# Transformer layer in 32 steps: a value half and a second-FFN piece trade places on TensorE, two low halves of squares move one slot later on VectorE

## The chip, the cores and the metric

The program runs on one core of one Trainium2 chip. The metric is the device time of one execution in microseconds (us), the median of several runs. The engines are named as in the profile: PE is TensorE's matrix multiply, PEld its load of the stationary operand, DVE is VectorE, ACT is ScalarE, POOL is GpSimd and SP the queue that issues transfers.

## What is computed

One transformer layer on 8 sequences of 1024 rows of width 512, with a sliding window of 256 keys, 16 heads of 32, and a feed-forward network (FFN) of 2048 hidden units whose weights are ternary and have a low-rank addition:

```python
x = L0_attn_x
x = x + _layernorm(_L0_attn_ref(_layernorm(x, axis=-1), Wq, bq, Wk, bk, Wv, bv, Wo, bo), axis=-1)
x = x + _layernorm(_L0_ffn_ref(_layernorm(x, axis=-1), fast_b, w_fc, w_proj, u, v, gate), axis=-1)
# _L0_ffn_ref:
h = _bitlinear(x, w_fc) + gate * (x @ v.T @ fast_b.T @ u.T)
r = jnp.maximum(h, 0.0)
return _bitlinear(r * r, w_proj)
```

## The kernel before

The 8192 rows are cut into 32 steps of 256 rows, four steps to a sequence; step t is the (t % 4)-th of its sequence, and the first of each sequence has no earlier keys. Every engine runs the same loop, `run_iterations`: iterations -2 to 34, each of 32 slots. A slot is the unit of order: in each slot every engine issues what the tables name for it, in the order in which its `body` is written, and the engines meet only through semaphores. The tables map a slot number of 0 to 95 to a piece of work; the number modulo 32 is the slot in which it runs, and the quotient says how many iterations after the work's base iteration. So one iteration holds work of several steps: the attention scores of step t, the query, key and value projections of step t+1, and the FFN of steps t-2 and t-3. `due(it, table, slot, lag, base)` yields the entries of a table that fall in this slot; a `lag` of 1 means one slot after the number in the table.

What PE does in a slot s, in this order: `scores` (L590, tile S) of block s; where there is one `weighted_values` (L624, tile Ob); `hidden_low_rank` (L716, tile F); `values` and `queries_keys` (L634, tile Ab; in the trace `Ab<-w_attn,xT` is a value half and `Ab<-xT,w_attn` a query or key half); `out_projection` (L634, Cb); `hidden` (L704, F); `ff_out` (L731, F), a piece of 8 matmuls of the second FFN product; and last `scores_transposed` (L606, tile Tb). I write S(s) and T(s) for the scores and the transposed scores that PE issues in slot s, V(0,0) and V(0,1) for the first and second half of the values of row block 0, ff(1,0) to ff(1,3) for the four pieces of row block 1, and QK(1,1) for the second half of head group 1.

The other parts that matter here:

- The queries, keys and values all go through one bank, Ab, one after the other: QK(1,0) and QK(1,1) in slots 31 and 1, then V(0,0) and V(0,1) in slots 3 and 5, then QK(2,0) in slot 7. Before V(0,0) may write, ACT must have read QK(1,1) out of the bank, which is `qk_bias` (L897, L899), in ACT's slot 2.
- ACT in a slot: `exponentials_transposed` (L870: it empties Tb of the slot before), `exponentials` (L852) of the block before, then the FFN's parts, `b_hi` (L906, the high part of the normalised and turned rows x2T of row block 0 in slot 2), and `qk_bias`. T(s) must not start before ACT has emptied Tb of T(s-1).
- DVE in a slot: evacuations, `masked_scores` (L1172) of block s, then `square_lo` (L1298), statistics (L1191, L1193, L1260) and normalisations. PE's S(s) needs the `masked_scores` of block s-2 done, since there are two S banks.
- The squares: for each pair m of 0 to 7, ACT writes `relu` (r32) and the high half of its square, POOL the full square (`square`, L1539, sq32), and DVE the low half (`square_lo`, L1298, reads sq32 and the high half). PE's piece ff(0,2) in slot 30 waits for m up to 5, ff(0,3) in slot 0 for m up to 7. The pieces of row block 1 wait for none of it, as they come later.
- The rows before the FFN: DVE normalises row block i (`y_norm` L1253, then POOL's residual L1534, `b_stats`, `b_norm` L1266) and turns it (`b_turn`, L1274, into sq32); SP sends it through DRAM (`x2_out` L399, `x2_in` L406, one queue, in order), and ACT and DVE split it (`b_hi`, `b_lo` L1279). `b_turn` of row block 0 (slot 29) waits for the low half of m = 6 of the FFN of the step before, as both use sq32. `low_rank` (L634, Cb<-x2T,v_T) waits for `b_lo` of both row blocks.

The lines that order V(0,0) behind ACT:

```python
elif t or pos > 1:
    need(pe, *a_freed(t, pos - (2 if t < 2 else 1)))
```

Of the kernel before, what the change touches and what calls it, by code (L numbers as in the profile page):

```python
# [55 lines left out]
A_STATS, STAT_OUT, STAT_IN = {36: 0, 38: 1}, {41: 0}, {44: 0}  # L56
A_NORM, A_SPLIT = {46: 0, 48: 1}, {50: 0, 52: 1}
QK_SLOT = {25: (0, 0), 29: (0, 1), 31: (1, 0), 33: (1, 1), 39: (2, 0), 41: (2, 1), 47: (3, 0), 49: (3, 1)}
V_SLOT = {35: (0, 0), 37: (0, 1), 43: (1, 0), 45: (1, 1)}
STACK_SLOT = {21: 0, 29: 1, 37: 2, 44: 3}  # L60

XR_SLOT = {19: 0, 20: 1}
# [2 lines left out]
Z_SLOT = {40: 0}  # L65
FF1_SLOT = {44 + 2 * m: m for m in range(8)}
FF2_PIECES = 4
FF2_SLOT = {59: (0, 0), 60: (0, 1), 62: (0, 2), 64: (0, 3), 66: (1, 0), 68: (1, 1), 70: (1, 2), 74: (1, 3)}

PIECES = 8  # L70
QK_EARLY = ({25: (0, 0), 26: (0, 1), 27: (1, 0), 28: (1, 1), 29: (2, 0), 30: (2, 1), 64: (3, 0), 65: (3, 1)},
# [13 lines left out]
def need(eng, sem, value):  # L85

    if isinstance(value, int) and value <= 0:
        return
    eng.wait_ge(sem, value)
# [31 lines left out]
def due(it, table, slot, lag, base, early=None, late=0):  # L121


    for back in range(3):
        if it.has(base - back):
            t, p = it.step(base - back)
            at = slot - lag + back * SLOTS
            entry = early[t].get(at - late) if early and t < 2 else table.get(at)
            if entry is not None:
                yield t, p, entry  # L130
# [9 lines left out]
def lagged(it, slot, lag):  # L140

    j = slot - lag
    back = 0 if j >= 0 else 1
    return (it.has(-back), *it.step(-back), j + back * SLOTS)
# [40 lines left out]
def steps(nc, A, W, out):  # L185

    with ExitStack() as ctx:
# [179 lines left out]
        def _(sp):  # L367
# [79 lines left out]
            def stack(t, p, hg):  # L447

                ring = 1 + p % (RING // STEP)
                sp.wait_ge(M[f"qk_out{hg}"], (t + 1) * 16)  # L450
                need(sp, M["T_full"], tiles_through(t - 1, (p - 1) % PER_SEQ, hg))
                pieces = qk_hop[hg].rearrange("(r i) (j n) -> i r j n", r=GROUP, n=STEP)
                for term, parts_of in enumerate(((0, 2), (0, 3), (1, 2))):
                    for block, j in zip((0, ring), parts_of):
                        sp.dma_start(QK3[term * HD:(term + 1) * HD, hg * GROUP:(hg + 1) * GROUP, block, :],
                                     pieces[:, :, j]).then_inc(M[f"stacked{hg}"], 16)

            def body(it):
                for s in range(SLOTS):
# [24 lines left out]
                    for t, p, hg in due(it, STACK_SLOT, s, 0, 1):  # L484
                        if t > 0:
                            stack(t, p, hg)
                    for t, p, (i, piece) in due(it, FF2_SLOT, s, 6, -1):
                        if piece == FF2_PIECES - 1:
# [15 lines left out]
        def _(pe):  # L504
# [134 lines left out]
            def values(t, i, half):  # L639
                if half == 0:  # L640
                    if t == 0:
                        pe.wait_ge(M["w_lo"], 3)
                    a_wait(pe, t, v_pos(t, i))
                    pe.wait_ge(M["a_xl"], t * TILES + i + 1)
                cols = slice(half * D // 2, (half + 1) * D // 2)
                mm = product3(a_bank(t, v_pos(t, i))[:, cols].rearrange("p (c n) -> p c n", c=2),
                              lambda a, k: turned_of(t)[:, a, k, i * P:(i + 1) * P],
                              lambda a, k: W["w"][:, 2, 2 * half:2 * half + 2, a, k, :])
                if half == 1:
                    mm.then_inc(M["A_full"], 1)  # L650
# [40 lines left out]
            def hidden(t, m):  # L691


                b = m % 2
                if t == 0 and m == 0:
                    pe.wait_ge(M["f_back"], 4 * PIECES)
                    pe.wait_ge(M["u_back"], 2)
                    pe.wait_ge(M["s2_done"], 1)
                need(pe, M[f"F_free{b}"], t * NF + m // 2)
                for half in range(2):  # L700
                    mc = 2 * m + half
                    for k in range(KD):
                        for part in range(2):
                            pe.matmul(Fb[b][:, half * STEP:(half + 1) * STEP],  # L704
                                      W["t1"][:, mc, k, :], x2T[:, part, k, :],
                                      start=(half == 0 and k == 0 and part == 0), stop=False,
                                      skip_group_check=True)

            def hidden_low_rank(t, m):

                if m == 0:
                    pe.wait_ge(M["z_done"], t + 1)
                b = m % 2
                for half in range(2):
                    mc = 2 * m + half
                    mm = pe.matmul(Fb[b][:, half * STEP:(half + 1) * STEP], W["u"][0:LR, mc * P:(mc + 1) * P],  # L716
                                   z6[:], start=False, stop=True, skip_group_check=True)
                mm.then_inc(M[f"F_full{b}"], 1)

            def ff_out(t, i, q):  # L720

                o = Fb[i]
                if q == 0:
                    pe.wait_ge(M[f"F_free{i}"], t * NF + 4)
                if i == 0:
                    pairs = t * (KH // 2) + (q + 1) * KH // 2 // FF2_PIECES
                    pe.wait_ge(M["r2_lo"], pairs)
                    pe.wait_ge(M["r2_hi"], pairs)
                for m in range(q * KH // FF2_PIECES, (q + 1) * KH // FF2_PIECES):
                    for part in range(2):  # L730
                        mm = pe.matmul(o[:, :], r2[:, part, m, i * P:(i + 1) * P], W["t2"][:, m, :],  # L731
                                       start=(m == 0 and part == 0), stop=(m == KH - 1 and part == 1),
                                       skip_group_check=True)
                if q == FF2_PIECES - 1:
                    mm.then_inc(M[f"F_full{i}"], 1)

            def body(it):
                for s in range(SLOTS):
# [27 lines left out]
                    for t, p, m in due(it, FF1_SLOT, s, 1, -1):  # L766
                        hidden_low_rank(t, m)
                    for t, p, (i, half) in due(it, V_SLOT, s, 0, 2, V_EARLY):
                        values(t, i, half)
# [6 lines left out]
                    for t, p, m in due(it, FF1_SLOT, s, 0, -1):  # L776
                        hidden(t, m)
                    for t, p, (i, piece) in due(it, FF2_SLOT, s, 0, -1):
                        ff_out(t, i, piece)
# [207 lines left out]
        def _(v):  # L987
# [300 lines left out]
            def z_last(t):  # L1288
                v.wait_ge(M["z_mid"], t + 1)
                need(v, M["F_full1"], t * NF - 1)  # L1290
                v.scalar_tensor_tensor(z6[:], z_m[:], W["zsel"][0:LR, 1:2], z_r[:], ALU.mult,
                                       ALU.add).then_inc(M["z_done"], 1)

            def square_lo(t, m):
                hi, lo = (r2[:, k, 2 * m:2 * m + 2, :].rearrange("p m n -> p (m n)") for k in range(2))
                v.wait_ge(M["r2_sq"], t * (KH // 2) + m + 1)
                v.wait_ge(M["r2_hi"], t * (KH // 2) + m + 1)
                v.tensor_tensor(lo, sq32[:, m % 2], hi, ALU.subtract).then_inc(M["r2_lo"], 1)  # L1298
# [18 lines left out]
            def body(it):  # L1317
                for s in range(SLOTS):
                    ok, t, p, j = lagged(it, s, LAG_SHIFT - 1)
                    if ok and j % 8 == 7:  # L1320
                        turn_shift(t, j // 8)
                    for t, p, (i, half) in due(it, V_SLOT, s, 1, 2, V_EARLY, 1):
                        if half == 1:
# [6 lines left out]
                    for t, p, (i, half) in due(it, WO_SLOT, s, 1, -1):  # L1330
                        if half == 1:
                            y_evacuate(t, i)
                    for t, p, (i, piece) in due(it, FF2_SLOT, s, 1, -1):
                        if piece == FF2_PIECES - 1:
                            c_evacuate(t, i)
                    ok, t, p, i = lagged(it, s, LAG_OT_LO)
# [8 lines left out]
                        z_rest(t)  # L1345
                    for t, p, _ in due(it, Z_SLOT, s, 4, -1):
                        z_last(t)
                    for t, p, m in due(it, FF1_SLOT, s, 4, -1):
                        square_lo(t, m)
                    for t, p, (i, half) in due(it, WO_SLOT, s, 2, -1):  # L1350
                        if half == 1:
                            y_stats(t, i)
                    for t, p, (i, piece) in due(it, FF2_SLOT, s, 2, -1):
                        if piece == FF2_PIECES - 1:
# [10 lines left out]
                    for t, p, i in due(it, B_STATS, s, 0, -1):  # L1365
                        b_stats(t, p, i)
                    for t, p, (i, piece) in due(it, FF2_SLOT, s, 4, -1):
                        if piece == FF2_PIECES - 1:
# [37 lines left out]
        def _(g):  # L1406
            def rstd(k, row, n):

                g.wait_ge(M[k + "_ve"], n + 1)
                g.tensor_tensor(lnrs[:, row, 0:1], lnve[:, row, :], W["nhalf"][:], ALU.pow).then_inc(M[k + "_rs"], 1)  # L1410
# [135 lines left out]
            def body(it):  # L1546
                for s in range(SLOTS):
# [21 lines left out]
                    for t, p, i in due(it, B_STATS, s, 1, -1):  # L1569
                        rstd("b", 2, t * TILES + i)  # L1570
                    for t, p, (i, piece) in due(it, FF2_SLOT, s, 3, -1):
                        if piece == FF2_PIECES - 1:
# [70 lines left out]
```

## Time and profile before

| | |
|---|---|
| median of 3 runs | 2284.57 us (2282.37 to 2287.46) |
| profiled execution | 2285.86 us |
| its span, first to last instruction | 2284.1 us |
| PE busy | 2191.4 us, 96% |
| DVE, ACT, POOL busy | 76%, 72%, 65% |
| granted TensorE clock, mean | 0.989 |
| from 205 to 2063 us: PE busy | 1852.42 of 1858.00 us |

Busy times are unions of the instructions of an engine. The execution has a start of some 200 us in which the weights are prepared beside the first iterations, a stretch from about 205 to 2063 us in which the iterations repeat (63.5 to 69 us each), and an end in which the attention of the last step and the FFN of the last steps run out. The profiled execution is the one that all rows below are from.

### The profile page before, as it was taken

What the parts mean: (1) busy time and instruction counts of PE and PEld (TensorE: products, weight loads), DVE (VectorE), ACT (ScalarE), POOL (GpSimd) and SP (SyncE); (2) the same over time, 40 slices, a digit from 0 to 9 for tenths busy, and PEclk for the clock granted to TensorE, in tenths of its full rate; (3) what the DMA queues carried; (4) which work ended last, traced back from release to release, by engine and by line L of the source; (5) the groups of instructions that cost most, each with busy time, mean ns of one, the idle gap of its engine ahead of it and who ended that gap; (6) DMA issues with size and microseconds to landing.
All of it is one profiled execution on the core that took longest, in us unless ns stands there. A gap on an engine that the chain in (4) does not pass through costs nothing.

```text
span 2284.1 us, 61076 instructions
## 1 busy us (share of the span) xinstructions
PE 2191.4 (96%) x20149; PEld 1655.8 (72%) x20149; DVE 1738.3 (76%) x4619; ACT 1637.0 (72%) x4647; POOL 1474.8 (65%) x2570
## 2 busy tenths in 40 slices
PE   4788999999999999999999999999999999999997
PEld 3556777777777777777777777777777777777664
DVE  7887777877778877777787777888778787786764
ACT  3787776777767776777767776677767777677752
POOL 4455666776666776666667666667766667675553
PEclk9899999999999999999999999999999999999999
DMA  6333233223333323333332232332233233322211
GB/s 222 122 94 96 82 94 102 79 90 102 91 96 96 90 76 103 102 88 95 92 94 88 88 101 87 104 92 83 86 101 108 79 97 92 88 82 75 60 39 37
DMA packets 230587, 210.80 MB, mean 92 GB/s; under 512 B 34928, under 2 KB 170096, under 8 KB 229248
## 3 DMA queue, kind: packets, MB, share of 16 engines
q1 hardware_dynamic: 227584, 198.51, 29.1%
q10 hardware_dynamic: 2688, 8.39, 1.0%
q8 instruction: 161, 2.64, 0.5%
q14 instruction: 154, 1.26, 0.2%
HBM read 137.53 MB, written 67.17 MB: 90 GB/s over the span
## 4 chain that ended last, share of the span: by engine, by line
PE 87%; DVE 5%; ACT 4%; issue 2%; DMA 1%; POOL 1%; SPq 0%; ACTq 0%; POOLq 0%; DVEq 0%
PE Ab L634 21%; PE F L704 19%; PE F L731 16%; PE Cb L634 9%; PE Ob L624 7%; PE Tb L606 6%; PE S L590 6%; PE F L716 3%; ACT Sm L852 1%; DVE Sm L1172 1%; ACT x2T L906 1%; ACT qk L899 0%; ACT qk L897 0%; ACT PT L870 0%; DVE r L1298 0%
## 5 line engine op out<-in xcount | busy, mean ns | idle before, releaser
L870 ACT ACTIVATE PT<-Tb 128x384 f32<-128x384 f32 x896 | 440.4, 491 | 442.5 <-PE Tb L606 438.6
L1172 DVE CUSTOM_DVE_ANT_0 Sm<-S,mask,scales 128x384 f32<-128x384 f32 (+2 forms) x1024 | 572.2, 561 | 219.6 <-PE S L590 212.5
L852 ACT ACTIVATE Sm<-Sm,nmax 128x384 f32<-128x384 f32 (+2 forms) x1024 | 584.5, 571 | 108.1 <-DVE nmax L1172 106.0
L704 PE MATMUL F<-x2T,t 128*128 128x256 f16 x4096 | 489.1, 272 | 0.0
L731 PE MATMUL F<-t,r 128*128 128x512 f16 x2048 | 482.0, 379 | 1.3 <-DVE r L1298 1.2
L704 PEld LDWEIGHTS F<-x2T,t 128*128 128x128 f16 x4096 | 397.9, 98 | 52.2
L634 PE MATMUL Ab<-xT,w_attn 128*128 128x256 f16 x2928 | 366.2, 276 | 4.3 <-DVE w_attn L1026 4.3
L731 PEld LDWEIGHTS F<-t,r 128*128 128x128 f16 x2048 | 197.4, 97 | 197.4 <-DVE r L1298 1.7
L590 PE MATMUL S<-QK 96*128 96x384 f16 (+2 forms) x1280 | 316.7, 280 | 8.7 <-DVE nmax L1172 5.9
L1410 POOL TENSOR_TENSOR lnrs<-lnve,nhalf 128x1 f32<-128x1 f32 x192 | 122.6, 638 | 310.7 <-DVE lnve L1260 127.3
L634 PEld LDWEIGHTS Ab<-xT,w_attn 128*128 128x128 f16 x2928 | 282.2, 99 | 55.3 <-issue 12.6
L606 PE MATMUL Tb<-QK 128*128 128x256 f16 (+1 forms) x1792 | 295.2, 246 | 17.6 <-ACT PT L870 15.9
L1522 POOL TENSOR_SCALAR_AFFINE_SELECT PT<-PT 128x256 f32<-128x256 f32 x512 | 241.3, 476 | 107.0 <-ACT PT L870 104.5
L1539 POOL TENSOR_TENSOR sq<-r 128x512 f32<-128x512 f32 x256 | 287.1, 1122 | 35.4 <-ACT r L922 34.5
L606 PEld LDWEIGHTS Tb<-QK 128*128 128x128 f16 x1792 | 172.0, 98 | 92.3 <-ACT PT L870 21.1
L922 ACT ACTIVATE r<-F,c 128x256 f32<-128x256 f32 x512 | 212.3, 468 | 17.2 <-PE F L716 15.2
L1298 DVE TENSOR_TENSOR r<-sq,r 128x512 f16<-128x512 f32 x256 | 207.9, 813 | 11.4 <-POOL sq L1539 11.4
L1519 POOL TENSOR_SCALAR_AFFINE_SELECT PT<-PT 128x256 f32<-128x256 f32 x384 | 182.8, 479 | 52.2 <-ACT PT L870 50.7
L852 ACT ACTIVATION_READ_ACCUMULATOR Sm<-Sm,nmax 128x1 f32 x1024 | 198.6, 194 | 0.0
L634 PE MATMUL Cb<-w_attn,OT 128*128 128x256 f16 x1560 | 193.0, 273 | 3.8 <-ACT qk L899 3.8
L634 PE MATMUL Ab<-w_attn,xT 128*128 128x256 f16 x1464 | 180.1, 273 | 9.3 <-ACT qk L899 9.3
L624 PE MATMUL Ob<-PT,V 128*32 128x128 f32 (+1 forms) x3584 | 174.3, 332 | 0.0
(199 smaller groups left out, 3285.1 us busy)
## 6 DMA issues: line engine op xcount, KB each, us to landing
QK<-qk_hop SPq DMA_DIRECT2D x768, 64.0 KB, 2.0
qk_hop<-qkp SPq DMA_DIRECT2D x128, 256.0 KB, 2.1
x<-in_x SPq DMA_DIRECT2D x64, 256.0 KB, 2.9
x_hop<-sq SPq DMA_DIRECT2D x256, 64.0 KB, 1.8
r<-x_hop SPq DMA_DIRECT2D x64, 256.0 KB, 2.7
out<-yb SPq DMA_DIRECT2D x64, 256.0 KB, 2.2
xa<-in_x SPq DMA_DIRECT2D x30, 512.0 KB, 3.8
xa<-in_xt SPq DMA_DIRECT2D x30, 512.0 KB, 4.4
```

The costliest lines, as they stand in the source:

```text
L590: mm = pe.matmul(Sb[j % 2][:, place * P:(place + n) * P], Q3[0:ST, h, qc * P:(qc + 1) * P], K3[0:ST, h, slot * P:(slot + n) * P], start=Tr ...
L606: mm = pe.matmul(Tb[:, col:col + width], K3[:, h, ring + key:ring + key + P], Q3[:, h, q0:q0 + width], start=True, stop=True, skip_group_c ...
L624: mm = pe.matmul(Ob[r * HD:(r + 1) * HD, q0:q0 + width], V[:, c, h * HD:(h + 1) * HD], src[:, blk * P:blk * P + width], start=(k == 0), st ...
L634: mm = pe.matmul(outp, a(pa, k), b(pb, k), start=(n == 0), stop=(n == 3 * KD - 1), skip_group_check=True)
L704: pe.matmul(Fb[b][:, half * STEP:(half + 1) * STEP], W["t1"][:, mc, k, :], x2T[:, part, k, :], start=(half == 0 and k == 0 and part == 0), ...
L731: mm = pe.matmul(o[:, :], r2[:, part, m, i * P:(i + 1) * P], W["t2"][:, m, :], start=(m == 0 and part == 0), stop=(m == KH - 1 and part == 1),
L852: act.activation(blk, blk, ACT.Exp, bias=nmax[:, hg % 2, j % 8:j % 8 + 1], scale=-1.0, accum_out=sums[:, hg % 2, j % 8:j % 8 + 1]).then_in ...
L870: act.activation(PT[:, tile % NPT].rearrange("p b n -> p (b n)"), Tb[:, 0:WIN], ACT.Exp, bias=1.0, scale=c_score).then_inc(M["T_exp"], 1)
L922: ins = act.activation(r32[:, b, half * STEP:(half + 1) * STEP], Fb[b][:, half * STEP:(half + 1) * STEP], ACT.Relu, scale=W["c1"][:, 2 * m ...
L1172: v.tensor_tensor_reduce(Sm[:, j % NSM, c0:WIN], Sb[j % 2][:, c0:WIN], W["mask"][:, c0:WIN], W["c"][:, 3:4], 3e38, ALU.add, ALU.min, nmax[ ...
L1522: g.affine_select(out=blk, in_=blk, compare_op=ALU.is_ge, fill=zero, base=0, pattern=[[0, 2], [1, P]], channel_multiplier=-1).then_inc(M[" ...
L1539: g.tensor_tensor(sq32[:, m % 2], r32[:, m % 2], r32[:, m % 2], ALU.mult).then_inc(M["r2_sq"], 1)
```

## The change

Two entries of the PE tables and the order of `square_lo` on DVE are changed. `V_SLOT` has the value half (0,0) at 36 in place of 35, so in slot 4. `FF2_SLOT` has the piece (1,1) at 67 in place of 68, so in slot 3. `LATE_LO` names the pairs 5 and 6, whose `square_lo` runs with a lag of 5 in place of 4: in slots 27 and 29 in place of 26 and 28. A line is added near the top, so every line number of the changed kernel is one higher up to the DVE body.

```diff
-V_SLOT = {35: (0, 0), 37: (0, 1), 43: (1, 0), 45: (1, 1)}
+V_SLOT = {36: (0, 0), 37: (0, 1), 43: (1, 0), 45: (1, 1)}
...
+LATE_LO = (5, 6)
-FF2_SLOT = {59: (0, 0), 60: (0, 1), 62: (0, 2), 64: (0, 3), 66: (1, 0), 68: (1, 1), 70: (1, 2), 74: (1, 3)}
+FF2_SLOT = {59: (0, 0), 60: (0, 1), 62: (0, 2), 64: (0, 3), 66: (1, 0), 67: (1, 1), 70: (1, 2), 74: (1, 3)}
...
+                    for t, p, m in due(it, FF1_SLOT, s, 5, -1):
+                        if m in LATE_LO:
+                            square_lo(t, m)
                     for t, p, m in due(it, FF1_SLOT, s, 4, -1):
-                        square_lo(t, m)
+                        if m not in LATE_LO:
+                            square_lo(t, m)
```

PE in the middle of the program, from S(2) to V(0,1), before. S<-QK opens each slot, F<-t,r is an ff piece and Ab<-w_attn,xT a value half:

```order
L590 MATMUL S<-QK 128x128
L731 MATMUL F<-t,r 128x512 x8
L606 MATMUL Tb<-QK 128x256
L606 MATMUL Tb<-QK 128x128
L590 MATMUL S<-QK 128x128
L634 MATMUL Ab<-w_attn,xT 128x256 x12
L606 MATMUL Tb<-QK 128x256
L606 MATMUL Tb<-QK 128x128
L590 MATMUL S<-QK 128x256
L731 MATMUL F<-t,r 128x512 x8
```

The same place in the changed kernel:

```order
L591 MATMUL S<-QK 128x128
L732 MATMUL F<-t,r 128x512 x8
L607 MATMUL Tb<-QK 128x256
L607 MATMUL Tb<-QK 128x128
L591 MATMUL S<-QK 128x128
L732 MATMUL F<-t,r 128x512 x8
L607 MATMUL Tb<-QK 128x256
L607 MATMUL Tb<-QK 128x128
L591 MATMUL S<-QK 128x256
L635 MATMUL Ab<-w_attn,xT 128x256 x12
```

The value half and the piece behind it have changed places: two ff pieces now follow each other, and the two value halves stand in slots 4 and 5.

DVE in the middle of the program, slots 26 to 29, before (r<-sq,r is `square_lo`; lnst, lnmv, lnve are `b_stats` of row block 0; yb<-yb is `y_norm` of row block 1; yb<-x is `b_norm` and sq<-yb `b_turn` of row block 0; Sm,nmax is `masked_scores`):

```order
L1298 TENSOR_TENSOR r<-sq,r 128x512
L1191 BN_STATS lnst<-x 128x6
L1193 BN_AGGR lnmv<-lnst 128x2
L1260 TENSOR_SCALAR lnve<-lnmv 128x1
...
L1253 TENSOR_SCALAR yb<-yb,lnmv,lnrs 128x512
L1172 ISA Sm,nmax<-S,mask,scales 128x384
L1172 ISA nmax 128x1
L1298 TENSOR_TENSOR r<-sq,r 128x512
L1266 TENSOR_SCALAR yb<-x,lnmv,lnrs 128x512
L1172 ISA Sm,nmax<-S,mask,scales 128x384
L1172 ISA nmax 128x1
L1274 STREAM_TRANSPOSE sq<-yb 128x4x4x32
```

The same place in the changed kernel:

```order
L1192 BN_STATS lnst<-x 128x6
L1194 BN_AGGR lnmv<-lnst 128x2
L1261 TENSOR_SCALAR lnve<-lnmv 128x1
...
L1299 TENSOR_TENSOR r<-sq,r 128x512
L1254 TENSOR_SCALAR yb<-yb,lnmv,lnrs 128x512
L1173 ISA Sm,nmax<-S,mask,scales 128x384
L1173 ISA nmax 128x1
L1267 TENSOR_SCALAR yb<-x,lnmv,lnrs 128x512
L1173 ISA Sm,nmax<-S,mask,scales 128x384
L1173 ISA nmax 128x1
L1299 TENSOR_TENSOR r<-sq,r 128x512
L1275 STREAM_TRANSPOSE sq<-yb 128x4x4x32
```

The low half of m = 5 has moved from ahead of `b_stats` to behind the next `masked_scores`, and that of m = 6 from ahead of `b_norm` to directly ahead of `b_turn`.

## Rows read from the trace of the kernel before

**Rows 1.** The page, busy time, share of the span and instructions.

```profile
PE 2191.4 (96%) x20149; PEld 1655.8 (72%) x20149; DVE 1738.3 (76%) x4619; ACT 1637.0 (72%) x4647; POOL 1474.8 (65%) x2570
```

**Rows 2.** Waits, 205 to 2063 us: us in total, times, longest.

```profile
PE Ab L634 <- ACT qk L899: 5.6, 28, 0.2
```

**Rows 3.** Timeline of PE, 1057 to 1064 us: start, length, idle before.

```profile
1057.17 1.89 PE L731 MATMUL F<-t,r 128*128 128x512 f16 x8
...
1059.07 0.33 PE L590 MATMUL S<-QK 96*128 96x384 f16 x1
1059.60 1.48 PE L634 MATMUL Ab<-w_attn,xT 128*128 128x256 f16 x12 [0.20 <-ACT qk L899]
...
1063.14 0.33 PE L590 MATMUL S<-QK 96*128 96x384 f16 x1
1063.31 1.47 PE L634 MATMUL Ab<-w_attn,xT 128*128 128x256 f16 x12
```

**Rows 4.** Chain of waits, 1058 to 1060 us: start, length.

```profile
1058.29 0.52 ACT x2T L906
1058.81 0.36 ACT qk L897
1059.17 0.37 ACT qk L899
```

**Rows 5.** Timeline of PE, first and last stalls of 28, and one of another kind.

```profile
255.30 1.48 PE L634 MATMUL Ab<-w_attn,xT 128*128 128x256 f16 x12 [0.20 <-ACT qk L899]
...
1127.70 0.22 PE L590 MATMUL S<-QK 96*128 96x128 f16 x1
1128.13 1.49 PE L634 MATMUL Ab<-w_attn,xT 128*128 128x256 f16 x12 [0.20 <-ACT qk L899]
...
2062.97 1.48 PE L634 MATMUL Ab<-w_attn,xT 128*128 128x256 f16 x12 [0.19 <-ACT qk L899]
```

**Rows 6.** Timeline of ACT, slot 3.

```profile
1059.43 0.49 ACT L870 ACTIVATE PT<-Tb 128x384 f32<-128x384 f32 x1
```

**Rows 7.** Timeline of DVE, slots 28 to 3 of one iteration.

```profile
1046.64 1.59 DVE L1298 TENSOR_TENSOR r<-sq,r 128x512 f16<-128x512 f32 x1
...
1048.70 0.60 DVE L1172 CUSTOM_DVE_ANT_0 Sm<-S,mask,scales 128x384 f32<-128x384 f32 x1
...
1053.81 0.62 DVE L1172 CUSTOM_DVE_ANT_0 Sm<-S,mask,scales 128x384 f32<-128x384 f32 x1 [0.79 <-PE S L590]
...
1061.19 0.61 DVE L1172 CUSTOM_DVE_ANT_0 Sm<-S,mask,scales 128x384 f32<-128x384 f32 x1
```

**Rows 8.** Timeline of PE, S(31) and S(0).

```profile
1050.12 0.33 PE L590 MATMUL S<-QK 96*128 96x128 f16 x2
...
1053.31 0.33 PE L590 MATMUL S<-QK 96*128 96x384 f16 x1
```

**Rows 9.** Timeline of PE, iteration 2, in the start.

```profile
188.57 1.48 PE L634 MATMUL Ab<-w_attn,xT 128*128 128x256 f16 x12 [1.33 <-ACT qk L899]
...
202.21 1.48 PE L634 MATMUL Ab<-w_attn,xT 128*128 128x256 f16 x12 [0.82 <-ACT qk L899]
```

**Rows 10.** Timeline of all engines in the end, 2226 to 2244 us.

```profile
2226.62 1.27 POOL L1534 TENSOR_TENSOR x<-yb,x 128x512 f32<-128x512 f32 x1
2226.69 1.74 DVE L1298 TENSOR_TENSOR r<-sq,r 128x512 f16<-128x512 f32 x1 [1.45 <-POOL sq L1539]
2228.35 1.26 DVE L1266 TENSOR_SCALAR yb<-x,lnmv,lnrs 128x512 f32<-128x512 f32 x1
2229.64 0.71 DVE L1274 STREAM_TRANSPOSE sq<-yb 128x512 f32<-128x512 f32 x1
2230.38 1.78 SPq L399 DMA_DIRECT2D x_hop<-sq  x4
...
2235.00 0.34 SPq L406 DMA_DIRECT2D r<-x_hop  x1
...
2243.08 2.76 PE L634 MATMUL Cb<-x2T,v_T 128*96 128x256 f16 x12 [5.01 <-DVE x2T L1279]
```

**Rows 11.** Timeline of DVE in the end, `b_stats` of row block 0 and `y_norm`.

```profile
2223.02 0.69 DVE L1298 TENSOR_TENSOR r<-sq,r 128x512 f16<-128x512 f32 x1
...
2224.63 0.15 DVE L1260 TENSOR_SCALAR lnve<-lnmv 128x1 f32<-128x1 f32 x1
```

## The prediction

> **What bounds the kernel now.** I read the page first, to see which engine is nearest to full: PE, with 96% of the span [rows 1], and DVE, ACT and POOL at 76% or less. Between 205 and 2063 us PE is busy in all but 0.3% of the time, so what one iteration takes is what PE issues in it, plus whatever stops PE. A gain in that stretch can only come from such a stop. So the second view is the list of waits, for PE alone, over the repeating stretch. It names one line for PE's own matmuls: Ab at L634 waits for ACT's qk at L899, 28 times [rows 2]. That is once in each of the 28 iterations between 205 and 2063 us, always at V(0,0) [rows 5].
>
> The third view is PE's timeline around one of them [rows 3]. Where nothing is late, a value half starts 0.17 us behind the scores ahead of it (1063.14 to 1063.31). V(0,0) starts 0.53 us behind S(3) (1059.07 to 1059.60). So the stop is 0.36 us; the 0.20 us in brackets is smaller because the end of a matmul is drawn past the start of the next. Where the scores are one matmul of 128 columns it is 0.43 us (1127.70 to 1128.13) against 0.17, so 0.26 us [rows 5].
>
> The chain of waits tells who makes PE late: ACT does `b_hi` (0.52 us), then the two halves of `qk_bias` (0.36 and 0.37), which end at 1059.54 [rows 4], and V(0,0) follows at 1059.60 [rows 3]. ACT was not idle there; between QK(1,1) and V(0,0) PE has only one piece of 1.9 us, ff(1,0) from 1057.17 to S(3) at 1059.07 [rows 3], and ACT's slot 2 takes longer than that.
>
> **The change, part by part.** Nothing is added or removed: the same matmuls, activations, DVE instructions and transfers run, so PE's work is the same and only stops can change.
>
> *V(0,0) and ff(1,1) trade places.* ff(1,1) reads squares that were done an iteration before and writes a bank that ff(1,0) already holds, so nothing keeps it from starting 0.17 us behind S(3), at 1059.24. A piece and its scores take what ff(1,0) took, 1.90 us to the next scores and 0.17 more. V(0,0) is then due at about 1059.24 + 2.06 = 1061.3, and ACT has the bank empty at 1059.54: a reserve of 1.8 us where 0.36 was lacking. The whole stop goes, for all 28: 21 of 0.36 and 7 of 0.26 us, 7.6 + 1.8 = 9.4; added up stop by stop, 9.3 us. I take 9.3.
>
> Who is late next, with the stop gone? T(3) must wait for ACT to empty T(2), and ACT does that behind `qk_bias`: from 1059.43 to 1059.92 [rows 6]. T(3) now follows ff(1,1), at about 1060.97: 1.0 us of reserve. Slots 4 and 5 are now both short, so S(5) comes 0.36 us earlier, at 1062.78 instead of 1063.14 [rows 3]; it needs the `masked_scores` of block 3, which DVE ran late, from 1061.19 to 1061.80 [rows 7]: reserve 1.0 us. The evacuation of the values on DVE waits for V(0,1), which ends earlier, not later. No SP or POOL instruction moves here.
>
> *In the start* (iterations 1 and 2) there is no FFN piece yet. The stops at V(0,0) are longer (1.33 us at 188.57 [rows 9], and another like it in iteration 1), but T(3) would then wait for the same busy ACT, and PE waits for ACT again at 202.21 for 0.82 us [rows 9]. I count nothing; the bound above is both stops whole, 2.8 us, the bound below nothing.
>
> *The low halves of m = 5 and 6 one slot later.* In the repeating stretch nothing of this reaches PE. ff(0,2) needs m = 5 only in slot 30, m = 5 runs in slot 27. The DVE instructions between slot 26 and `b_turn` are the same set, so it ends about when it did, give or take one collision: `square_lo` of m = 6 took 1.59 us at 1046.64 [rows 7] where one that met nothing took 0.69 [rows 11]. The long ones stand beside POOL's residual, as at 2226.62 and 2226.69 [rows 10]: DVE's instruction ends about 0.6 us after POOL's. Moved, `square_lo` leaves that place to `b_norm` and may meet POOL's next square instead. If both are held, DVE is 0.9 us later at `masked_scores` of block 30. What covers this: `masked_scores` of block 29 ended at 1049.30 [rows 7] and S(31) came at 1050.12 [rows 8], 0.8 us of reserve, and block 29 now comes ahead of the low half; S(0) is at 1053.31 [rows 8], and DVE sat idle for 0.79 us ahead of 1053.81 [rows 7]. Cost: nothing.
>
> The Trainium skill, "SBUF — State Buffer", section "Who interferes with whom", says that a DVE instruction with two SBUF inputs and a GpSimd instruction that reads SBUF exclude each other, and likewise a DVE `tensor_scalar` in a two-port mode; whichever is first has the pair for its whole length. By that rule the move only chooses which DVE instruction is held, and would speak against a gain in the steady stretch; the trace agrees with the hold (the 1.59 and 1.74 us above).
>
> *The end* is the one place where this part counts. The last `low_rank` stood idle for 5.01 us, until 2243.08, for x2T [rows 10]. Its chain is one SP queue: `x2_out` of row block 0 at 2230.38, `x2_in` at 2235.00, then the same for row block 1. It begins when `b_turn` ends (2229.64 + 0.71 = 2230.35). Ahead of that DVE ran m = 5 (from 2223.02) and then `b_stats` of row block 0 (its last instruction at 2224.63 [rows 11]), and POOL's rstd, its square of m = 6 and the residual hang behind that. DVE then waited 1.45 us for the square, was held 1.1 us by the residual (1.74 against 0.69), and `b_norm` took 1.26 us [rows 10]. Changed, `b_stats` comes 0.6 us earlier (the length of one low half), POOL's queue with it, and `b_norm` fills DVE's wait instead of following it: 1.26 us at most, of which I take 1.1. Together 1.7 us earlier; every later step of that queue moves with it. Bounds: 0 (if collisions eat it) and 1.9.
>
> **Sum.** 9.3 + 1.7 + 0 = 11.0 us. The profiled execution took 2285.86 us, 1.3 more than the median of its runs: 2274.9 from the one, 2273.6 from the other. I say 2274.2.
>
> **Rivals.** *(a) A new wait takes part of it.* With slots 4 and 5 short, one of the two reserves of 1.0 us may be smaller in some kind of iteration; if half of each stop comes back, the gain is 4.7 + 1.7 = 6.4 us: 2278.2. Against it: both reserves are nearly three times the 0.36 us by which PE comes earlier.
> *(b) The stop only moves.* If V(0,0) was late for another reason than the qk bank (the list names the releaser that came last), it would wait in slot 4 too, and only the end's gain is left, 2282.9. Against it: PE starts 0.06 us after L899 ends, 28 times with the same 0.19 or 0.20 us.
> *(c) Slower.* DVE is already late at block 3, and runs without a pause up to there. If the move of m = 6 pushes DVE's queue past the 0.79 us of idle in slot 0 by more than 1.0 us, S(5) waits for it in every iteration. It decides from a delay of 1.8 us in all; to be 0.2% (4.6 us) slower it must also eat the 9.3 + 1.7: (11.0 + 4.6)/28 = 0.56 us more, 2.35 us. Time then 2289. Against it: the collisions give 0.9 us at most.
> *(d) Larger.* The stops in the start are saved too: 2.8 more, 2271.4.
>
> **How the numbers follow.** Forecast 0.74 (2271.5 to 2277, from the runs' own spread of about 2.5 us to either side), (d) 0.06, (a) 0.10, (b) 0.06, (c) 0.04. The range 2269.0 to 2280.0 holds the forecast, (d) and (a). A measurement of this kernel can tell about 0.2%, 4.6 us, from no change: the forecast, (d) and most of (a) are faster, 0.87; (b) and a little of (a) the same, 0.09; (c) slower, 0.04.
>
> **What would show it.** Right: the list of waits for PE in the repeating stretch has no Ab <- ACT qk; V(0,0) starts 0.17 us behind S(4); the iterations are 0.26 or 0.36 us shorter; PE's idle ahead of the last `low_rank` ends some 1.7 us sooner relative to the last S; `b_stats` stands ahead of the low half. Wrong: a wait of PE for nmax at S(5), for PT at T(3) or T(4), or for qk still at V(0,0); or DVE's pause in slot 0 gone and L1172 of block 3 late.

## The result and the profile after

The changed kernel took 2275.76 us (median of 6 runs, 2273.44 to 2277.74); the kernel before, on the same chips, 2287.06 us (6 runs, 2282.37 to 2287.95). The ratio is 0.9954, with a 95% interval of 0.9941 to 0.9967: faster, by some 10.5 us (7.5 to 13.5 by the interval; the two medians differ by 11.3). The profiled execution has a span of 2274.3 us against 2284.1, and took 2276.04 us.

The page of the changed kernel, span and busy time:

```profile
span 2274.3 us, 61076 instructions
PE 2189.0 (96%) x20149; PEld 1658.9 (73%) x20149; DVE 1768.0 (78%) x4619; ACT 1638.8 (72%) x4647; POOL 1482.6 (65%) x2570
```

PE's work is the same to 2.4 us [rows 1]; DVE is busy for 30 us more with the same number of instructions, of which more below. The waits of the changed kernel between 205 and 2053 us (total, times, longest), all that are PE's:

```profile
PEld Ob L625 <- issue: 21.6, 89, 0.4
PEld F L717 <- issue: 11.1, 56, 0.2
PEld Ab L635 <- issue: 10.9, 55, 0.2
PEld Ob L625 <- POOL PT L1524: 5.0, 22, 0.3
```

No line with "PE" is left: only weight loads, which overlap the matmuls, show a pause, and the 28 waits of Ab for ACT's qk [rows 2] are gone. The timeline of PE in the same place of the iteration as [rows 3] (start, length):

```profile
1053.65 0.33 PE L591 MATMUL S<-QK 96*128 96x384 f16 x1
1053.82 1.89 PE L732 MATMUL F<-t,r 128*128 128x512 f16 x8
1055.54 0.33 PE L607 MATMUL Tb<-QK 128*128 128x256 f16 x2
1055.71 0.33 PE L591 MATMUL S<-QK 96*128 96x384 f16 x1
1055.87 1.47 PE L635 MATMUL Ab<-w_attn,xT 128*128 128x256 f16 x12
```

S(3) at 1053.65 is followed by ff(1,1) after 0.17 us, and V(0,0) follows S(4) after 0.16 us. ACT, in the timeline of that place, is no faster than before:

```profile
1052.78 0.62 ACT L907 ACTIVATE x2T<-r 128x512 f16<-128x512 f32 x1
1053.30 0.46 ACT L898 ACTIVATE qk<-Ab,bqs 128x256 f32<-128x256 f32 x1
1053.65 0.47 ACT L900 ACTIVATE qk<-Ab,bqs 128x256 f32<-128x256 f32 x1
1054.01 0.49 ACT L871 ACTIVATE PT<-Tb 128x384 f32<-128x384 f32 x1
```

It still empties the bank at 1054.12, which is 0.47 us after S(3), but V(0,0) now needs it only at 1055.87, 1.75 us later; and T(3) at 1055.54 comes 1.04 us after ACT has emptied T(2) (1054.01 + 0.49).

**Where the time went.** The first matmul of `low_rank` (Cb<-x2T,v_T) marks each of the 32 steps. Its first and 29th start in the timeline of the kernel before, which frame 28 iterations:

```profile
197.02 1.47 PE L634 MATMUL Cb<-x2T,v_T 128*96 128x256 f16 x12
...
2073.58 1.47 PE L634 MATMUL Cb<-x2T,v_T 128*96 128x256 f16 x12
```

and in the changed kernel:

```profile
196.07 1.47 PE L635 MATMUL Cb<-x2T,v_T 128*96 128x256 f16 x12
...
2062.21 1.47 PE L635 MATMUL Cb<-x2T,v_T 128*96 128x256 f16 x12
```

So the repeating stretch takes 1876.56 and 1866.14 us. Start to start, the iterations in it took 62.6 to 69.0 us before (not from 63.5, as the section on the time before has it) and take 62.2 to 68.6 now; each of the 28 is shorter by 0.36 to 0.38 us. With the last three starts and the span I cut every profiled execution of this study into six parts (us; each is the difference of two starts; "behind" is from the last `low_rank` to the end of the span):

| execution | until step 0 | 28 iterations | steps 28-29 | 29-30 | 30-31 | behind |
|---|---|---|---|---|---|---|
| before | 197.02 | 1876.56 | 64.03 | 59.05 | 46.42 | 41.02 |
| before_again | 198.66 | 1876.69 | 64.02 | 59.10 | 46.54 | 42.59 |
| changed | 196.07 | 1866.14 | 64.57 | 59.86 | 45.20 | 42.46 |
| after_again | 198.22 | 1866.23 | 64.57 | 59.88 | 45.14 | 41.16 |
| e1_swap_only | 199.23 | 1866.20 | 64.02 | 59.13 | 46.42 | 41.40 |
| e2_late_only | 196.11 | 1877.11 | 64.59 | 59.62 | 44.43 | 41.14 |
| e3_value_only | 196.60 | 1887.75 | 64.03 | 59.05 | 46.49 | 42.48 |
| e4_bias_first | 194.85 | 1866.15 | 64.03 | 59.08 | 46.38 | 42.11 |
| e5_late_last | 197.57 | 1866.46 | 64.01 | 59.13 | 44.77 | 41.46 |
| e6_keep_clock | 198.83 | 1866.34 | 64.01 | 59.12 | 44.96 | 39.74 |
| e7_double_before | 198.04 | 1891.02 | 64.01 | 60.04 | 46.30 | 41.39 |
| e8_double_after | 201.22 | 1866.43 | 64.58 | 59.87 | 44.82 | 41.48 |

The two kernels ran twice each. Between the two executions of a kernel the four middle parts repeat to 0.15 us; the first part and the last do not, and differ as much between two executions of one kernel as between the kernels. By the middle parts the change gives 10.4 to 10.5 us in the 28 iterations, loses 0.54 and 0.81 behind them, and gives 1.2 to 1.4 in the interval before the last `low_rank`: 10.3 us in all in the first pair of executions, 10.5 in the second.

### The profile page after: what moved, and what is told of

The parts are those of the page before. It is cut to its first block, busy times and chain, and to the rows that moved or that the text cites. A ratio compares the mean times of both kernels' runs of the same rounds, so it can differ in the third digit from the quotient of the medians.

```text
span 2274.3 us, 61076 instructions
## 1 busy us (share of the span) xinstructions
PE 2189.0 (96%) x20149; PEld 1658.9 (73%) x20149; DVE 1768.0 (78%) x4619; ACT 1638.8 (72%) x4647; POOL 1482.6 (65%) x2570
## 4 chain that ended last, share of the span: by engine, by line
PE 90%; DVE 5%; issue 2%; ACT 2%; DMA 1%; POOL 1%; SPq 0%; POOLq 0%; DVEq 0%; ACTq 0%
PE Ab L635 21%; PE F L705 19%; PE F L732 18%; PE Cb L635 9%; PE Ob L625 7%; PE Tb L607 6%; PE S L591 6%; PE F L717 3%; DVE Sm L1173 1%; ACT Sm L853 0%; DVE w_attn L1027 0%; ACT PT L871 0%; DVE yb L1016 0%; DVE r L1299 0%; DVE turned L1183 0%
## 5 line engine op out<-in xcount | busy, mean ns | idle before, releaser
L1544 POOL TENSOR_TENSOR sq<-r 128x512 f32<-128x512 f32 x256 | 295.3, 1154 | 35.4 <-ACT r L923 34.5
```

Of the source, the lines that this page charges most:

```text
L1544: g.tensor_tensor(sq32[:, m % 2], r32[:, m % 2], r32[:, m % 2], ALU.mult).then_inc(M["r2_sq"], 1)
```

## The experiments

**e1_swap_only: the exchange on PE alone.**

```diff
-V_SLOT = {35: (0, 0), ...
+V_SLOT = {36: (0, 0), ...
-FF2_SLOT = {... 68: (1, 1), ...
+FF2_SLOT = {... 67: (1, 1), ...
```

> Only the two PE slots are exchanged, square_lo keeps its old slots. Theory 1 (the PE exchange alone removes the stop at V(0,0), DVE's part never reaches PE in the repeating stretch): the 28 repeating iterations are shorter by 0.37 us each as in the changed kernel, 10.4 us, no new wait of PE there; in the last two iterations with scores the loss of 0.54 and 0.81 us seen in the changed kernel shrinks to 0 and 0.3, since ff(0,3) no longer waits for DVE. Time 11 us below before. Theory 2 (the later low halves are what makes room on DVE for the exchange): PE waits for nmax or for DVE's r in the repeating stretch, and at least 3 us of the 10.4 are missing.

Measured: 2277.18 us (ratio 0.9961, interval 0.9948 to 0.9973). The 28 iterations take 1866.20 us, with no wait of PE in them, and the two intervals behind are back at 64.02 and 59.13. Theory 2 falls: DVE's later low halves are not needed for the exchange.

**e2_late_only: the later low halves alone.**

```diff
+LATE_LO = (5, 6)
...
+                    for t, p, m in due(it, FF1_SLOT, s, 5, -1):
+                        if m in LATE_LO:
+                            square_lo(t, m)
                     for t, p, m in due(it, FF1_SLOT, s, 4, -1):
-                        square_lo(t, m)
+                        if m not in LATE_LO:
+                            square_lo(t, m)
```

> Only the low halves of m = 5 and 6 are a slot later, PE's order is that of before. Theory 1: the stop of 0.37 us at V(0,0) stays in all 28 iterations, none of the 10.4 us comes; the last two iterations with scores lose 0.5 us each, and b_turn of row block 0 in the end comes 1.4 us earlier, which the lower clock behind it may take back; time within 2 us of before. Theory 2 (DVE's order feeds ACT earlier, so ACT is less late at qk): the stop shrinks by 0.1 us or more per iteration, 3 us or more in all.

Measured: 2287.4 us against 2285.62 of the kernel before (ratio 1.0006, interval 0.9996 to 1.0016). Its list of waits from 205 to 2055 us, which leaves out the last of the 28 stops:

```profile
PE Ab L635 <- ACT qk L900: 5.9, 27, 0.8
```

The stop at V(0,0) is there as before, once 0.8 us long; the 28 iterations take 1877.11, half a microsecond more and not less. The loss of 0.56 and 0.57 us behind them is there, and so is a shorter last interval: 44.43 us against 46.42, of which 1.38 us is the earlier `b_turn` (see "The end" below). So this part of the change gives nothing in the repeating stretch and little outside it.

**e3_value_only: V(0,0) in slot 4, ff(1,1) left there too.**

```diff
-V_SLOT = {35: (0, 0), ...
+V_SLOT = {36: (0, 0), ...
```

> Only V(0,0) moves to slot 4; ff(1,1) stays in slot 4 behind it, so slot 3 holds only scores and transposed scores. Theory 1 (what counts is the 2 us of PE work put between QK(1,1) and its bank's next use): T(3) comes due at once but must wait for ACT to empty T(2), which stands behind qk_bias and ends at 0.85 us after S(3), so a stop of 0.6 to 0.75 us takes the place of the 0.37, and the kernel is 6 to 11 us slower than before. Theory 3 (V(0,0) was merely one slot too early, its cover does not matter): the stop goes, 10 us faster.

Measured: 2297.85 us, ratio 1.0054 (1.0037 to 1.0071), slower. PE's timeline, slot 3 and the beginning of slot 4:

```profile
1063.79 0.33 PE L590 MATMUL S<-QK 96*128 96x384 f16 x1
1064.70 0.34 PE L606 MATMUL Tb<-QK 128*128 128x256 f16 x2 [0.58 <-ACT PT L870]
1064.87 0.33 PE L590 MATMUL S<-QK 96*128 96x384 f16 x1
1065.04 1.48 PE L634 MATMUL Ab<-w_attn,xT 128*128 128x256 f16 x12
```

V(0,0) stops no more, but T(3) starts 0.91 us behind S(3), where 0.17 is the undisturbed distance: a stop of 0.74 in place of 0.37, and 1887.75 - 1876.56 = 11.2 us over the 28 iterations, 0.40 each, just above the 6 to 11 expected (12.2 us by the medians). ACT's slot 2 is the late part, whichever PE instruction asks for it first; what removes the stop is the piece of 2 us in between.

**e4_bias_first: the kernel before with ACT's two parts exchanged, in every slot.**

```diff
-                    for t, p, i in due(it, B_NORM, s, 6, -1):
-                        b_hi(t, i)
                     for t, p, (hg, w) in due(it, QK_SLOT, s, 1, 2, QK_EARLY, 1):
                         if w == 1:
                             qk_bias(t, hg)
+                    for t, p, i in due(it, B_NORM, s, 6, -1):
+                        b_hi(t, i)
```

> The kernel before, but ACT does qk_bias ahead of b_hi in each slot; PE and DVE keep their orders. Theory 1 (V(0,0) waits for the qk bank, which ACT empties late because b_hi of 0.52 us stands ahead of qk_bias): qk_bias ends 0.52 us earlier, the stop of 0.37 goes without any move on PE, 10 us faster than before. Theory 4 (V(0,0) waits for something else that ends at the same time, and the list names the last releaser only): the stop stays, no gain.

Measured: 2274.68 us (ratio 0.9956, 0.9939 to 0.9972), as fast as the change, with PE's order of before. The 28 iterations take 1866.15 us, the same number to 0.01 us. ACT in slot 2:

```profile
1051.56 0.46 ACT L897 ACTIVATE qk<-Ab,bqs 128x256 f32<-128x256 f32 x1
1051.92 0.47 ACT L899 ACTIVATE qk<-Ab,bqs 128x256 f32<-128x256 f32 x1
1052.28 0.63 ACT L906 ACTIVATE x2T<-r 128x512 f16<-128x512 f32 x1
```

PE's S(3) was at 1052.44 and V(0,0) at 1052.60, 0.16 behind. `qk_bias` ended at 1052.39, just before. Its list of waits from 205 to 2055 us has no line of PE. That the same 1866.2 us comes out of a move on PE and of one on ACT speaks for its being PE's own work, with no stop left.

**e7_double_before and e8_double_after: the suspected cost doubled.** Both add an ACT copy of 0.52 us ahead of `b_hi` for row block 0, to a tile that nothing reads, in the kernel before and in the changed one (the lines that make the tile and its semaphore are left out here):

```diff
...
+                if i == 0:
+                    need(act, M["extra"], t)
+                    act.activation(spare[:], landed(i), ACT.Copy).then_inc(M["extra"], 1)
                 act.activation(x2_blocks(0, i), landed(i), ACT.Copy).then_inc(M["b_xh"], 1)
```

> The kernel before, with one more ACT copy of the size of b_hi ahead of it for row block 0, to a tile that nothing reads. Theory 1: qk_bias ends 0.52 us later, the stop at V(0,0) grows from 0.37 to 0.89 us, 14.6 us slower over the 28 iterations. Theory 4 (V(0,0) waits for something else): much less than that.

> The changed kernel with the same added ACT copy of 0.52 us. Theory 1 with the reserves as predicted (1.8 us at V(0,0), 1.0 us at T(3)): no stop, 1866.15 us again over the repeating stretch. If the reserve at T(3) is smaller than 0.52 us, a wait for PT appears there, up to 0.5 us per iteration, 15 us.

Measured: before with the copy 2300.13 us (ratio 1.0062, 1.0047 to 1.0077), changed with the copy 2277.16 us (0.9961, 0.9946 to 0.9976). The 28 iterations of the first grew by 1891.02 - 1876.56 = 14.5 us, 0.52 each; those of the second are 1866.43 against 1866.14 and 1866.23. So before the change what is added on ACT ahead of `qk_bias` is paid in full by PE, and after it 0.52 us more costs at most 0.3 us over all 28 iterations: the reserve is at least 0.52 us. PE in the first kernel:

```profile
1066.28 0.33 PE L591 MATMUL S<-QK 96*128 96x384 f16 x1
1067.33 1.48 PE L635 MATMUL Ab<-w_attn,xT 128*128 128x256 f16 x12 [0.72 <-ACT qk L900]
```

1.05 us behind S(3), a stop of 0.88.

**e5_late_last: the exchange, and the later low halves for the last two steps alone.**

```diff
-                        if m in LATE_LO:
+                        if m in LATE_LO and t >= NSTEP - 2:
...
-                        if m not in LATE_LO:
+                        if m not in LATE_LO or t < NSTEP - 2:
```

> The changed kernel, but the low halves of m = 5 and 6 run a slot later only for the last two steps (30 and 31). Theory 1: the repeating stretch stays at its 1866.15 us from the low_rank of step 0 to that of step 28; the two intervals behind it go back from 64.57 and 59.86 to 64.0 and 59.1 us, since ff(0,3) no longer waits for DVE; the last interval keeps the earlier b_turn, 45.2 us or less against 46.4. Time 1.2 us below the changed kernel, give or take 1.4 us of the TensorE clock behind the last idle stretch. Rival: the last interval gains only if the steps before it have the late order too, then it is 46.4 and nothing is won.

Measured: 2277.46 us (ratio 0.9966, 0.9952 to 0.9979). By parts it is what was expected: 64.01 and 59.13 without the loss, and 44.77 with the gain, 1.7 us less than the changed kernel in these three; the median does not show it (it is 1.7 us above the changed kernel's of 2275.76, from another round), since 1.7 us is below what the medians tell apart. The rival falls: the earlier `b_turn` does not need the steps before.

**e6_keep_clock: the kernel of e5 with 20 matmuls more ahead of the last `low_rank`.** Their result is not used.

```diff
+                if t == NSTEP - 1:
+                    pe.wait_ge(M["T_exp"], tiles_before(NSTEP, 0))
+                    for n in range(20):
+                        pe.matmul(Tb[:, :], W["t2"][:, n % KH, 0:P], W["t2"][:, n % KH, :], start=True, stop=True,
+                                  skip_group_check=True)
```

> The kernel of the run above with 20 matmuls of 128x512 added (their result is not used) ahead of the last low_rank, where PE is idle for 5 us. Clock theory: low_rank and the piece behind it take 2.8 and 2.0 to 3.4 us in place of 1.5 and 1.9 because PE's idle let the granted clock fall to 0.5; with PE kept busy until 0.6 us ahead of low_rank they take 1.5 and 1.9, and the end is 1.4 to 2.8 us shorter than without. Rival: the lengths come from late data or from the idle's last moment, and the added matmuls change nothing, or delay low_rank.

Measured: 2273.07 us (ratio 0.9942, 0.9929 to 0.9956), the lowest median of the study. Against the changed kernel's 0.9954 the intervals overlap; against e5, which differs by the added matmuls alone, its five runs (2269.07 to 2274.91 us) lie below all five of e5's (2275.12 to 2278.16). PE's timeline in the end of the changed kernel:

```profile
2231.84 2.77 PE L635 MATMUL Cb<-x2T,v_T 128*96 128x256 f16 x12 [4.95 <-DVE x2T L1280]
2234.40 3.39 PE L732 MATMUL F<-t,r 128*128 128x512 f16 x8
```

and with the added matmuls:

```profile
2228.39 4.48 PE L690 MATMUL Tb<-t 128*128 128x512 f16 x20
2233.26 1.48 PE L635 MATMUL Cb<-x2T,v_T 128*96 128x256 f16 x12 [0.40 <-DVE x2T L1285]
2234.58 1.89 PE L737 MATMUL F<-t,r 128*128 128x512 f16 x8
```

The granted clock stands in the column PEclk of the windows over these two groups, first of the changed kernel (stretch, its length, busy time and instructions of PE, PEld, DVE, ACT, POOL, then PEclk):

```profile
2231.90:2234.40 2.50, 2.50 (x13) 2.32 (x14) 0.00 (x0) 0.00 (x0) 0.00 (x0) 0.50 0.00 0
2234.40:2237.60 3.20, 3.20 (x9) 1.18 (x8) 0.48 (x1) 0.80 (x2) 0.00 (x0) 0.53 0.00 0
```

then with the added matmuls:

```profile
2233.30:2234.60 1.30, 1.30 (x13) 1.29 (x14) 0.00 (x0) 0.00 (x0) 0.00 (x0) 1.00 0.00 0
2234.60:2236.30 1.70, 1.70 (x10) 0.77 (x8) 0.48 (x1) 0.80 (x2) 0.00 (x0) 1.00 0.00 0
```

After 5 us without work the same twelve matmuls run at 1.2 GHz (0.50) in place of 2.4 and take 2.8 us in place of 1.5. The part behind is 39.74 us, 1.3 to 2.9 less than in any other execution and 1.72 less than in e5. The medians of e5 and e6 differ by 4.4 us; the 2.7 us beyond that stay open.

**after_again and before_again: both kernels once more, unchanged.**

> The changed kernel once more, to see what one execution's parts vary by. If the 0.95 us by which the start was shorter belongs to the change, the low_rank of step 0 comes at about 196 us again and in the kernel before at 197; if it is chance, they differ by a microsecond or more in either direction. The same for the end behind the last low_rank, 42.46 against 41.02 us.

> The kernel before once more, for the same: the repeating stretch 1876.56 us again to 0.1 us, the start 197 us and the part behind the last low_rank 41.0 us only if these are no chance.

Measured: 2275.35 us (ratio 0.9955, 0.9938 to 0.9971) and one run of 2289.35 us. The start comes at 198.22 and 198.66 us, where the first executions had 196.07 and 197.02; over all twelve it lies between 194.85 and 201.22 in no order that follows the edits. And before_again has the slow last piece that I had taken for an effect of the change:

```profile
2245.01 2.76 PE L634 MATMUL Cb<-x2T,v_T 128*96 128x256 f16 x12 [5.14 <-DVE x2T L1279]
2247.56 3.51 PE L731 MATMUL F<-t,r 128*128 128x512 f16 x8
```

That last piece takes 3.51 us here and took 1.97 in the first execution of the same kernel.

## Why the prediction was right, and where its terms were off

**What bounds the kernel, and who is late.** Right. PE's only own stop in the repeating stretch was V(0,0) waiting for ACT's qk. e4 removes it from ACT's side, e7 lengthens it by exactly what it adds to ACT, and e8 shows that the changed order no longer passes it on.

**The size of the stop.** The term was 9.3 us and measured 10.4. The step that was off is the 0.26 us that I gave to 7 of the 28 stops: I took the 0.17 us of a wide score product as the undisturbed distance where the scores are one matmul of 128 columns. The undisturbed distance there is shorter, as the timeline of the kernel before has it one slot earlier:

```profile
1125.75 0.22 PE L590 MATMUL S<-QK 96*128 96x128 f16 x1
1125.81 0.38 PE L731 MATMUL F<-t,r 128*128 128x512 f16 x1
```

0.06 us. With it the narrow stops are 0.43 - 0.06 = 0.37 [rows 5], as long as the others, and 28 times 0.37 is 10.4.

**The reserves.** Predicted 1.8 us at V(0,0) and 1.0 at T(3); the trace after has 1.75 and 1.04. At S(5) I expected 1.0; S(5) came at 1057.35, and DVE's `masked_scores` of block 3 ended at 1056.39:

```profile
1055.78 0.61 DVE L1173 CUSTOM_DVE_ANT_0 Sm<-S,mask,scales 128x384 f32<-128x384 f32 x1
```

0.96 us. Rivals (a) and (b) did not come about.

**The start.** I counted nothing. The stop of 1.33 us in iteration 2 [rows 9] did turn into one of T(3) for ACT:

```profile
188.01 0.34 PE L607 MATMUL Tb<-QK 128*128 128x256 f16 x2 [1.72 <-ACT PT L871]
```

The first part of the table varies by over 6 us between executions, so neither a gain nor a loss of a few microseconds there can be told from it. This one stop was not saved; whether rival (d), 2.8 us, holds for any part of the start stays open.

**The later low halves in the repeating stretch: "Cost: nothing".** Right for the 28 iterations (e2 loses 0.5 us in all, e1 without them equals the change). But DVE pays: its 30 us of added busy time are instructions held longer. DVE's slots 27 to 31 in the changed kernel (timeline):

```profile
1039.38 1.26 DVE L1254 TENSOR_SCALAR yb<-yb,lnmv,lnrs 128x512 f32<-128x512 f32 x1
...
1041.10 1.33 DVE L1267 TENSOR_SCALAR yb<-x,lnmv,lnrs 128x512 f32<-128x512 f32 x1
...
1042.88 1.36 DVE L1299 TENSOR_TENSOR r<-sq,r 128x512 f16<-128x512 f32 x1
...
1048.39 0.62 DVE L1173 CUSTOM_DVE_ANT_0 Sm<-S,mask,scales 128x384 f32<-128x384 f32 x1 [0.26 <-PE S L591]
```

In the same place before, `b_norm` met nothing:

```profile
1048.16 0.62 DVE L1266 TENSOR_SCALAR yb<-x,lnmv,lnrs 128x512 f32<-128x512 f32 x1
```

`b_norm` now takes 1.33 us in place of 0.62, and the low half of m = 6 still 1.36: both are held, as the case "if both are held" said, and DVE's pause in slot 0 shrank from 0.79 us [rows 7] to 0.26. Rival (c) thus came 0.53 us of the 1.8 it needed.

**The same part just behind the repeating stretch.** Here the step "Cost: nothing" failed. The prediction looked at ff(0,2), which needs m = 5, and left out ff(0,3) in slot 0, which needs m up to 7. In the repeating stretch nothing comes of it: in the changed kernel the low half of m = 7 ends at 1046.18 and ff(0,3) starts at 1048.06, with a query or key half of 1.5 us between. In the last iterations with scores the next step's projections are gone and PE comes sooner: before, m = 7 ended at 2183.28 and ff(0,3) started at 2183.48, a reserve of 0.2 us, and the later order makes DVE later than that. The last scores and the piece behind them, in the changed kernel's timeline of PE:

```profile
2170.41 0.33 PE L591 MATMUL S<-QK 96*128 96x384 f16 x1
...
2173.05 1.90 PE L732 MATMUL F<-t,r 128*128 128x512 f16 x8 [0.61 <-DVE r L1299]
```

ff(0,3) waits for DVE's low half. The loss is 0.54 and 0.81 us; e2 has 0.56 and 0.57 of it without the exchange, e5 has none (0.08 at most) without the late order there, and the exchange alone (e1) adds no more than 0.08. The 0.24 us more in the second interval come only with both parts together; there a T waits 0.85 us for the transfer of `QK<-turned`, which it does for 0.67 us in e1 and not at all in e2. No run takes this apart.

**The end.** The term was 1.7 us for `b_turn`; it measured 1.38. To see this, count from DVE's last `yb<-Cb`, an instruction that stands 24.0 us behind the `low_rank` of step 30 in both kernels. Before:

```profile
2220.67 0.75 DVE L1241 SCALAR_TENSOR_TENSOR yb<-Cb,scales,bo_rows 128x512 f32<-128x512 f32 x1 [1.82 <-PE Cb L634]
...
2224.87 0.78 POOL L1410 TENSOR_TENSOR lnrs<-lnve,nhalf 128x1 f32<-128x1 f32 x1 [0.75 <-DVE lnve L1260]
```

The changed kernel, timelines of DVE, POOL and all engines:

```profile
2210.65 0.75 DVE L1242 SCALAR_TENSOR_TENSOR yb<-Cb,scales,bo_rows 128x512 f32<-128x512 f32 x1 [1.81 <-PE Cb L635]
...
2214.22 1.03 POOL L1415 TENSOR_TENSOR lnrs<-lnve,nhalf 128x1 f32<-128x1 f32 x1 [0.53 <-DVE lnve L1261]
...
2215.29 1.17 DVE L1267 TENSOR_SCALAR yb<-x,lnmv,lnrs 128x512 f32<-128x512 f32 x1
2216.14 1.44 POOL L1539 TENSOR_TENSOR x<-yb,x 128x512 f32<-128x512 f32 x1
2216.38 1.75 DVE L1299 TENSOR_TENSOR r<-sq,r 128x512 f16<-128x512 f32 x1
2218.24 0.71 DVE L1275 STREAM_TRANSPOSE sq<-yb 128x512 f32<-128x512 f32 x1
```

`b_turn` starts 8.97 us behind that instruction before (2229.64 [rows 10] less 2220.67) and 7.59 us behind it now (2218.24 less 2210.65). It is 8.97 or 8.98 in all six executions without the late order in the end and 7.59 or 7.60 in all six with it. The mechanism is the one predicted, and its larger half came whole: `b_turn` follows the low half's end by 0.11 us in place of 1.21. The smaller half did not: `b_stats` does come 0.6 us earlier, but of that only 0.29 is left at the end of POOL's residual, as POOL's rstd takes 1.03 in place of 0.78 us and the residual 1.44 in place of 1.27, both beside a DVE instruction that has moved there.

DVE's low half ends at 2218.13, 0.55 us after POOL's residual (2217.58), as it did in [rows 10]: most of its work seems to be done only when POOL is through. The Trainium skill, "SBUF — State Buffer", section "Who interferes with whom", has this as an exclusive lock for the whole of an instruction, and the rows agree; no run here changed POOL's instruction to test it.

The rest of the last interval is the way of the rows through DRAM, from `b_turn` to the last `low_rank`. It takes 12.83 to 13.60 us over the twelve executions, 13.44 and 13.56 in the kernel before, 13.60 and 13.54 in the changed one, 12.83 in e2. This is why the interval shrank by 1.22 or 1.40 us here, and by 2.0 in e2, with the same 1.38 at `b_turn`.

One sign that the prediction named did not come about: PE's idle ahead of the last `low_rank` was to end 1.7 us sooner relative to the last S. It ends 61.48 us behind it before (2243.08 [rows 10] less 2181.60, in this line of PE's timeline) and 61.43 in the changed kernel (2231.84 less 2170.41); 61.65 and 61.39 in the second pair.

```profile
2181.60 0.34 PE L590 MATMUL S<-QK 96*128 96x384 f16 x1 [0.18 <-DVE nmax L1172]
```

The stop of ff(0,3) lies between the two and takes back what `b_turn` gives; in e5, which has not that stop, it is 59.91. What the first executions then showed behind the last `low_rank`, 1.4 us lost, is not the change's: before_again has it as well, and after_again has not.

**The sum.** Predicted 11.0 = 9.3 + 1.7 + 0; by parts 10.4 + 1.4 - 1.35 = 10.4 to 10.5 us, and 10.3 or 10.5 with what the way through DRAM took. The stop gave 1.1 us more than its term, the end 0.3 less, and the term put at nothing cost 1.35: these errors are opposite in sign and hid each other in the time. That the total came within 1 us of the forecast is luck; that nearly all of it is the stop at V(0,0) is not.

## What to carry to other kernels

When the bounding engine is full but for one stop per iteration, measure the stop as start-to-start against the same pair of shapes elsewhere undisturbed, multiply, and look which of its neighbours can stand in between: here the order on the waiting engine and the order on the late engine were worth the same, 10.4 us over 28 iterations. Once no stop is left, further moves should give nothing there; no run here made both moves at once. A reserve read in the repeating stretch does not hold in the last iterations, where half of the bounding engine's work is missing; check a moved instruction there by itself. Cut both executions at the same instruction into parts before explaining a difference of a few microseconds, and run each kernel twice, so that the parts that vary by chance are known.

## What the runs showed of the hardware that was not expected

One idle stretch of about 5 us ahead of the last `low_rank` costs a different amount in each execution. The twelve matmuls behind it take 2.04 to 2.77 us and the next eight 1.97 to 3.51 in the eleven executions that have it, against 1.48 and 1.89 where PE was kept busy. In the first 2 us of them the granted clock is 0.50 in seven executions and 0.55 to 0.68 in four (e1, e5, e7, e8), so it rises sooner in some than in others. From the first of the twelve to the end of the eight it is 4.52 to 6.06 us, and 3.21 in e6; what follows, to the end of the span, is 36.50 to 36.59 us in all twelve. So the whole variation of the part behind (41.02 to 42.59, and 39.74 in e6) lies in these twenty matmuls.

The undisturbed distance from a score product to the next matmul is 0.17 us for 384 columns but 0.06 us for one matmul of 128, so one figure cannot serve for both.

In the rows of the end POOL's rstd, an instruction of 128x1, takes 0.55 us at the shortest and 0.78 to 1.03 us in other places, and which place is long changes with DVE's order. What holds it was not tested.
